# The second normalisation of an attention layer: from VectorE to ScalarE, with a bias made on GpSimd

## The reference, cut to what matters

```
def _layernorm(x, axis=-1, eps=1e-05):
    m = jnp.mean(x, axis=axis, keepdims=True)
    v = jnp.var(x, axis=axis, keepdims=True)
    return (x - m) / jnp.sqrt(v + eps)
...
x = _layernorm(x + _L0_attn_ref(x, wq, wk, wv), axis=-1)
x = _layernorm(x + _L0_xattn_ref(x, ctx, ctx, mask, Wq, bq, Wk, bk, Wv, bv, Wo, bo), axis=-1)
x = _layernorm(x + _L0_ffn_ref(x, router_w, router_b, w1, b1, w2, b2), axis=-1)
```

## Time and profile before

| what | value |
|---|---|
| median of 3 runs | 2111.25 us (2110.53 to 2116.4) |
| the profiled execution: its own time | 2115.66 us |
| its span | 2113.5 us |
| its mean granted TensorE clock | 0.978 of full speed |
| PE, DVE, ACT, POOL busy | 95%, 69%, 49%, 46% |
| DVE's 128 instructions of L1092 (both normalisations) | 66.3 us |

### The profile page before, as it was taken

How to read it: one execution, slowest core, us unless ns; L and a number is a source line. 1 busy time by engine, 2 the same in 40 slices (tenths; PEclk the granted TensorE clock), 3 DMA queues, 4 the chain that set the end, 5 groups by cost and what they waited for, 6 DMA issues and landing times. The chain is left out here.

```text
span 2113.5 us, 55811 instructions
## 1 busy us (share of the span) xinstructions
PE 2015.6 (95%) x21785; PEld 1497.6 (71%) x21787; DVE 1452.1 (69%) x3052; ACT 1028.7 (49%) x1619; POOL 965.2 (46%) x1266
## 2 busy tenths in 40 slices
PE   7899999999999999999999999998789999999996
PEld 4667777777777777777677777665557878778785
DVE  5678877878877878877878877876415455554546
ACT  1455555555555555555555555554313242333433
POOL 3333444444444444444444444443335545455454
PEclk7899999999999999999999999999799999999998
DMA  3331112111101101101001101000023134332363
GB/s 97 100 114 53 44 35 72 52 54 38 39 29 41 31 29 33 37 25 32 26 26 33 36 26 32 26 27 17 21 78 76 31 88 91 72 83 38 88 234 147
DMA packets 99538, 118.86 MB, mean 56 GB/s; under 512 B 12144, under 2 KB 92221, under 8 KB 97232
## 3 DMA queue, kind: packets, MB, share of 16 engines
q1 hardware_dynamic: 69856, 83.75, 12.4%
q0 software_dynamic: 17184, 19.66, 5.1%
q10 hardware_dynamic: 12240, 11.88, 1.7%
HBM read 66.11 MB, written 56.12 MB: 58 GB/s over the span
## 5 line engine op out<-in xcount | busy, mean ns | idle before, releaser
L1009 DVE TENSOR_REDUCE smax<-ps_s 128x4 f32<-128x1024 f32 x508 | 619.1, 1219 | 206.7 <-PE ps_s L678 195.4
L885 ACT ACTIVATE prob<-ps_e 128x1024 f32<-128x1024 f32 x508 | 520.1, 1024 | 465.5 <-PE ps_e L691 326.5
L678 PE MATMUL ps_s<-stack_kh,stack_q 32*128 32x256 f32 x2032 | 304.3, 306 | 0.8 <-ACT stack_q L874 0.8
L691 PE MATMUL ps_e<-stack_q,stack_kh 32*128 32x256 f32 x2032 | 293.2, 281 | 0.0
L691 PE MATMUL ps_e<-stack_q,stack_kl 32*128 32x256 f32 x2032 | 289.9, 277 | 0.0
L1950 PE MATMUL m_ps_o<-w_sb,hid 128*128 128x256 f32 x1280 | 285.6, 379 | 1.2 <-DVE m_res L2075 1.2
L678 PE MATMUL ps_s<-stack_kl,stack_q 32*128 32x256 f32 x2032 | 275.6, 278 | 0.0
L1950 PEld LDWEIGHTS m_ps_o<-w_sb,hid 128*128 128x128 f32 x1280 | 240.1, 190 | 34.3 <-DVE m_res L2075 1.6
L718 PE MATMUL ps_w<-prob,val 128*32 128x256 f32 x4096 | 252.1, 387 | 1.2 <-ACT prob L885 1.2
L1274 POOL TENSOR_TENSOR padded<-m_rows 128x512 f32<-128x512 f32 x64 | 81.6, 1274 | 311.1 <-issue 226.3
L691 PEld LDWEIGHTS ps_e<-stack_q,stack_kl 32*128 32x128 f32 x2032 | 199.5, 188 | 0.0
(11 more groups left out here) (191 smaller groups left out, 4226.1 us busy)
## 6 DMA issues: line engine op xcount, KB each, us to landing
w_sb<-in_w SPq DMA_DIRECT2D x16, 1024.0 KB, 8.0
slot_rows_dram<-w_sb ACTq DMA_DIRECT2D x40, 258.0 KB, 2.8
m_rows<-slot_rows_dram SPq DMA_DIRECT2D x15, 645.0 KB, 4.9
xT<-in_xT SPq DMA_DIRECT2D x32, 256.0 KB, 3.0
ctxT<-in_ctxT SPq DMA_DIRECT2D x32, 256.0 KB, 2.9
x_res<-in_x SPq DMA_DIRECT2D x32, 256.0 KB, 2.9
sums_dram<-x SPq DMA_DIRECT2D x32, 256.0 KB
c_rows<-sums_dram SPq DMA_DIRECT2D x8, 1024.0 KB, 14.1
```

What stands on the lines that cost most here:

```text
L678: return nc.tensor.matmul(out, stack_q[at_side][rows, g, t * P:(t + 1) * P], (stack_kh, stack_kl)[part][at_side][rows, g, :], start=(X == ...
L691: return nc.tensor.matmul(out, (stack_kh, stack_kl)[part][at_side][rows, g, t * P:(t + 1) * P], stack_q[at_side][rows, g, :], start=False, ...
L885: nc.scalar.activation(prob[:, h:h + 2, :].rearrange("p h s -> p (h s)"), shifted[:, :, :, :].rearrange("p h t s -> p (h t s)"), ACT.Exp, ...
L1009: nc.vector.tensor_reduce(max_columns(X, p), scores[:, :, :, :], AX.X, ALU.max)\
```

## The change

The second normalisation leaves DVE's queue and enters ACT's. Before, DVE computed (y2 - mean) * rstd with the mean and rstd as per-row operands. After, ACT computes Identity(rstd * y2 + moved), with moved = -mean * rstd. POOL makes `moved` by two small instructions of 128x2: `minus_mean` between `veps` and `rstd`, and `moved` behind `rstd` with a wait. The first normalisation stays on DVE. The waits of `second_normed` on the readers of `x2` go with it to ACT.

```diff
@@ scalar
+            def second_normed(b):
...
+                act.wait_ge(ln_r[CROSS].sem, ln_r[CROSS].count(b))
+                for t in range(T2):
+                    nc.scalar.activation(x2[:, t, :], y2[:, t, :], ACT.Identity, bias=moved[:, t:t + 1],
+                                         scale=rstd[CROSS][:, t:t + 1]).then_inc(ln[CROSS].sem, 1)
...
                     elif m == DUOS // 2 and e is not None:
                         out_columns(*e, 0)
+                    if is_of(CROSS, q) and m == 0:
+                        second_normed(q[1])
@@ vector
-            def second_normed(b):
...
-                normalise(CROSS, b, y2, x2)
...
-                    if is_of(CROSS, q) and k == 1:
-                        second_normed(q[1])
@@ gpsimd, inverse_deviation
                 nc.gpsimd.tensor_scalar(veps[X][:, :], mv[X][:, :, 1], EPS, None, ALU.add).then_inc(ln_r[X].sem, 1)
-                pool.wait_ge(ln_r[X].sem, ln_r[X].count(b, 1))
+                if X == CROSS:
+                    nc.gpsimd.tensor_scalar(minus_mean[:, :], mv[X][:, :, 0], -1.0, None, ALU.mult).then_inc(ln_r[X].sem, 1)
+                pool.wait_ge(ln_r[X].sem, ln_r[X].count(b, 1 if X == SELF else 2))
                 ready()
                 nc.gpsimd.tensor_tensor(rstd[X][:, :], veps[X][:, :], minus_half[:, :], ALU.pow).then_inc(ln_r[X].sem, 1)
+                if X == CROSS:
+                    pool.wait_ge(ln_r[X].sem, ln_r[X].count(b, 3))
+                    ready()
+                    nc.gpsimd.tensor_tensor(moved[:, :], minus_mean[:, :], rstd[X][:, :], ALU.mult).then_inc(ln_r[X].sem, 1)
```

More of the change, by code:

```diff
@@ L218, in attend @@
         minus_half = sb("minus_half", [P, T2])
+        minus_mean = sb("minus_mean", [P, T2])
+        moved = sb("moved", [P, T2])
         x1 = [sb(f"x1_{parity}", [P, T2, D]) for parity in range(2)]
@@ L309, in attend @@
         ln = both("ln", 12, 11)
-        ln_r = both("ln_r", 2)
+        ln_r = both("ln_r", 2, 4)
         col_mm = both("col_mm", 1)
@@ L928, in gates @@
                 nc.scalar.activation(grown[:, :, :], below[:, :, :], ACT.Exp).then_inc(grew.sem, 1)
+            def second_normed(b):
+                if x2_sent.due(b - 1):
+                    act.wait_ge(x2_sent.sem, x2_sent.count(b - 1))
+                if x2T_mm.due(b - 1):
+                    act.wait_ge(x2T_mm.sem, x2T_mm.count(b - 1))
+                if rows_sent.due(b - 1):
+                    act.wait_ge(rows_sent.sem, rows_sent.count(b - 1))
+                act.wait_ge(ln_r[CROSS].sem, ln_r[CROSS].count(b))
+                for t in range(T2):
+                    nc.scalar.activation(x2[:, t, :], y2[:, t, :], ACT.Identity, bias=moved[:, t:t + 1],
+                                         scale=rstd[CROSS][:, t:t + 1]).then_inc(ln[CROSS].sem, 1)
             def rows_to_send(b):
@@ L1086, in mean_and_variance @@
                     nc.vector.bn_aggr(mv[X][:, t, :], st[:, t, :]).then_inc(s.sem, 1)
[L1088 to L1093, removed]
             def divide(X, b, t):
@@ L1122, in first_normed @@
                     dve.wait_ge(x1b_made.sem, x1b_made.count(b - 2))
-                normalise(SELF, b, y, x1[b % 2])
+                dve.wait_ge(ln_r[SELF].sem, ln_r[SELF].count(b))
+                for t in range(T2):
+                    nc.vector.tensor_scalar(x1[b % 2][:, t, :], y[:, t, :], mv[SELF][:, t, 0:1], rstd[SELF][:, t:t + 1],
+                                            ALU.subtract, ALU.mult).then_inc(ln[SELF].sem, 1)
             def second_norm(b):
```

## The result

The changed kernel takes 2135.14 us (median of 4 runs, 2130.01 to 2138.84), the kernel before 2111.11 us. The ratio is 1.0098 with a 95% interval of 1.0082 to 1.0114: 0.98% slower, by the ratio 20.7 us (0.0098 of 2111.11), between 17.3 and 24.1. The two medians by themselves lie 24.0 us apart, at the upper end of that; in its later series the kernel before had medians of 2113.9 to 2115.6 us. The forecast said slower, by 15.9 us. The direction and the mechanism were right; the size was some 5 us short, and the median lies 2 us above the stated range of 2116 to 2133 us.

A forecast was written before the change was run, and what follows sets the result against it. PE was taken to be paced by DVE's queue, tied to ACT's max_high at max_low; 13.9 + 1.0 + 0.6 + 0.4 = 15.9 us on the median 2111.25 gave 2127.2 us, range 2116 to 2133.

The forecast's parts named there:

- What paces the half-step: Attention-stage half-step of the change: PE is paced by DVE's queue, with true waits of 0.19 and 0.53 us at slots 3 and 4.
- the tie at `max_low`: DVE reaches max_low 0.03 us after ACT's max_high ends, so removing DVE's 1.38 us was costed at zero.
- ScalarE's price: Two activations between outT and slot 1's exponentials: 0.98 us of ACT's queue, from L1972, making the exponentials 0.58 us late.
- How often: 28 half-steps with a second normalisation: 24 lose 0.58 us each (13.9 us), four lose 0.26 each (1.0 us).
- The four half-steps of another kind: Those at 300, 662, 1025 and 1387, with slot 1's duo late and larger ACT idle time: 0.26 us each.
- POOL's part: minus_mean and moved add at most 0.66 us, hidden with 0.55 us to spare; 0.6 us once at the attention stage's end.
- The signs: Profile signs: exponentials 1.5 us behind outT, DVE idle 0.8 before max_low, PEld 0.3 more before slots 2 and 3.
- The rest: 29th to 31st second normalisations, where the pipeline runs out: 0.4 us for all, between 0 and 1.8.
- A: Rival on ACT's activations: ScalarE's cheap form, the pair taking 0.63 us, total 2117.4 us; chance 0.09.
- B: Rival at slots 3 and 4: max_low's delay is absorbed, so not slower, 2111 to 2113 us; chance 0.06.
- C: Rival: DVE's relief reaches PE, 0.27 us faster in each of 24 half-steps, 6.5 us, so 2104.8; chance 0.05.
- D: Rival: moved comes late and ACT waits for POOL, slower still; 0.3 us beyond the margin gives 2135.6; chance 0.04.

The follow-up runs named there:

- e2: The kernel before with the second normalisation left out on every engine, y2 itself being stored, transposed and sent; ratio 0.9993.
- e3: The changed kernel with the two activations replaced by plain copies of y2, the waits the same; ratio 1.0050 against the kernel before.
- e12: The change for the first 28 sequences, the last four as before (VectorE normalises, no bias on GpSimd); ratio 1.0062 against the kernel before.
- e10: The kernel before with only max_high of slot 1 put ahead of the exponentials of slot 1; VectorE still normalises; ratio 1.0012.
- e11: The change with max_high of slot 1 first, activations behind slot 1's exponentials; last four sequences as before; ratio 0.9971 against the kernel before.
- e5: The changed kernel with a third activation of the same kind behind the two; ratio 1.0207 against the kernel before.
- e1: The kernel before with GpSimd's minus_mean and moved added, their result unused, but VectorE's wait covering them; ratio 1.0096.
- e9: The changed kernel with one of the two activations given back to VectorE, which waits for rstd alone; ratio 1.0028 against the kernel before.
- e6: The changed kernel with both activations one place later in ScalarE's queue, behind max_high of slot 1; ratio 1.0045 against the kernel before.
- e8: The kernel before with GpSimd's two bias instructions behind rstd, result unused, and VectorE waiting for rstd alone; ratio 1.0015.

## Why the prediction was right, and where it was short

**What paces the half-step.** Shown. The reading of PEld's idle time against DVE's queue was right, and so was the tie at `max_low`: e2 confirms that 1.38 us less on VectorE is worth nothing.

**ScalarE's price.** The row of the last stage carried over: L1972 had 588 ns, the new activations have this:

```profile
L941 ACT ACTIVATE x<-y,moved,rstd 128x256 f32<-128x256 f32 x64 | 35.0, 596 | 6.9 <-POOL moved L1329 6.9
```

The pair takes 807.58 - 806.59 = 0.99 us of the queue. The step "they can start when `outT` is through, 0.55 us after its start" was off: it is 0.48 (806.11 to 806.59). That makes 0.52 us of delay and not 0.58, 12.2 us and not 13.9 in the 24. The Trainium skill's figure in "VectorE: DVE Perf Modes" (the TRN2 errata), by which an activation of 256 columns would take some 0.40 us (an estimate), does not hold for this form: 596 ns here. The Trainium skill's page "ScalarE: Activation LUTs", section on what ACT_TABLE_LOAD costs, has a plain activation at 186 ns plus 0.833 ns per column and some 93 ns more for each operand that is read per row, by estimate 585 ns; this trace agrees with that, and so does e3, in which a pair without the two operands loses 0.37 us less.

**How often.** The four half-steps of another kind were taken at 0.26 us each. Three of the four lost less: with the change I is 8.96 in them too, against 8.77, which is 0.19. The one that remains of another kind has 9.24 and lost 0.47. In all 1.0 us, as forecast, but by luck. With the intervals between, which grew by 1.0 us for a reason that was not looked for, the 28 half-steps lost 14.4 us, forecast 14.9.

**POOL's part.** Right for the 28 half-steps, with the bias ready 0.45 us early, forecast at least 0.55.

**The signs.** As stated beforehand, the exponentials of slot 1 start 1.5 us behind `outT` (806.11 to 807.58), DVE idles ahead of `max_low` for `max_high` (0.69 us, forecast 0.8), and ACT does not wait for `moved` in the 28 half-steps. PEld's idle time grew by 0.31 us ahead of slot 2, as said, but by 0.18 and not 0.3 ahead of slot 3.

**The step that was mis-sized** is the end of the stage and what follows it: "The rest", with 0.4 us for the 29th to 31st normalisation, and 0.6 us for POOL. The profiled executions have 4.8 us there and 3.5 us in the experts behind it; e12 puts some 7.6 us on the last four normalisations. The traces show these parts.

GpSimd's chain cost more than was taken. From the last `veps` to the end of the last scatter it is 22.96 us before the change and 24.21 after, 1.25 us more and not 0.6. All kernels without the bias in the last four (before, e2, e10, e11, e12) have 22.96 to 23.01 us, those with it 24.18 to 24.25, but for e5 with 29.58. Of the 1.25 us, some 0.7 are the two instructions with their waits. The other 0.5 us are idle time ahead of the first scatter (1524.20 in the earlier trace rows), 0.72 us against 0.19:

```profile
1543.22 1.12 POOL L1413 DMA_INDIRECT slot_rows_dram<-send,slot_u  x1 [0.72 <-issue]
```

Of the 3.5 us in the experts, 2.1 lie at the very end of the program, ahead of the first of the last ten scatters of the result. Before and after:

```profile
2094.15 1.18 POOL L1820 DMA_INDIRECT out<-m_res,m_token  x1 [0.18 <-issue]
```

```profile
2116.60 1.11 POOL L1827 DMA_INDIRECT out<-m_res,m_token  x1 [2.33 <-issue]
```

This idle time is 2.19 to 2.40 us in all nine kernels that make the bias for all 32 sequences (the change, e1, e3 to e9), and 0.18 in the five others. Why a few small instructions in the stage before bring it is not known. Another 1.2 us lie at the start of the experts (18.98 us to the same instruction and not 17.80, at a granted clock of 0.82 and not 0.90).

A wait in DVE's queue changed its owner: `divide` of an item waits for the normalisation of the item before it (`ln[CROSS].count(b - 1)`). As long as self items stand between, that is long done. At the end of the stage cross items follow each other, and this wait, once on work of DVE's own, is now on ACT:

```profile
1528.92 0.58 ACT L896 COPY outT<-ps_w 128x512 f32<-128x512 f32 x1 [3.73 <-PE ps_w L720]
1529.40 1.09 ACT L941 ACTIVATE x<-y,moved,rstd 128x256 f32<-128x256 f32 x2
```

```profile
1530.63 0.26 DVE L1117 RECIPROCAL rden<-ps_w 128x16 f32<-128x16 f32 x1 [5.56 <-ACT x L941]
```

Little of the 5.56 us is its doing, since the division also needs TensorE's product from `outT`. The division starts 1.71 us behind `outT` here; in e11, at the same granted clock of 1.00 and with VectorE normalising, it is 1.33 us and put down to PE:

```profile
1507.34 0.26 DVE L1122 RECIPROCAL rden<-ps_w 128x16 f32<-128x16 f32 x1 [0.67 <-PE ps_w L731]
```

So this wait costs 0.38 us, once. In the half-step shown in the first section, `max_low` stands 4.13 us behind `veps` and not 3.55, so that ScalarE's delay is there as in the steady part.

What is left goes with the clock. That same half-step takes 15.1 to 15.7 us in the eight kernels in which its granted clock is 1.00, 17.1 to 18.1 in the three with 0.90 or 0.91, 19.6 in e5 with 0.83, and 21.7 and 22.0 in the change and e6 with 0.69. e3 and e8, which also have added work in it, take 15.7 and 15.5. The stretch where the pipeline runs out differs from kernel to kernel by more than its own edits explain (149.7 us in e3, 167.1 in e5), and the longer ones have the lower granted clock there (e5 0.82, the change 0.87, before 0.88, e11 0.90). That the edits cause the lower clock is not shown, only that it goes with them, so how the 7.6 us divide as a whole stays open.

**The rivals.** A fell by e3, B by the rows above (the 0.51 us of `max_low` reach the duos of slots 3 and 4 whole), C by e2, and D by the trace, as ACT does not wait for `moved` in the 28 half-steps.

## What to carry to other kernels

Work moved from a busier engine to an idler one is priced by its place in the new queue, not by either engine's load: ask which instruction stands behind it and who waits for that, and look for idle time ahead of that very instruction. Where two engines came to a meeting point within 0.03 us of each other, relief of one was worth nothing, and only both edits together gained. A pipeline's last steps have other neighbours than its steady ones, so a moved instruction needs a second look there, and can keep its old place there.

## What the runs showed of the hardware

VectorE's normalisation from SBUF to SBUF (128x256, float32) and GpSimd's `x1b` hold each other up; the one that starts second gets longer. The pair of normalisations takes 0.73 or 0.74 us when no GpSimd instruction lies beside it. Where `x1b` has started first, the first of the two takes 0.69 to 1.28 us in the kernel before and ends 0.15 to 0.16 us after `x1b` in all 31 cases, and the second takes its usual 0.40; `x1b` itself keeps its 1.26 to 1.29 us. Where VectorE starts first, in e8, `x1b` takes 1.45 us in most cases. So 0.64 us of the 1.38 that the prediction counts as VectorE's own work were spent beside `x1b`. VectorE's maxima, which read PSUM, take 1.22 or 1.23 us beside `x1b` in e8, as elsewhere.

Executions of one kernel differ with the granted clock: e8's ten runs go from 2113.5 us at a mean clock of 0.982 to 2122.1 us at 0.976. So a difference of 3 us between two kernels needs many runs, while I is read to 0.02 us from one profile.
